# Moving the value products to the PSUM bank of the turned rows, and the residual behind the row sums, in a cross-attention and expert-layer kernel

## The reference

```python
q = layernorm(x) @ Wq + bq                     # 16 heads of 32
k, v = ctx @ Wk + bk, ctx @ Wv + bv            # 77 positions a batch
attn = softmax(clip(q k^T / sqrt(32), -1e4, 1e4))
x = x + (attn @ v) @ Wo + bo
weights = softmax over the top 2 of layernorm(x) @ expert_embeddings^T
each expert: its first 1024 rows with a weight, out = relu(rows @ W1^T) @ W2^T, times the weight
x = x + the experts' outputs, added into their rows
```

## Time and profile before

| | |
|---|---|
| time of the runs shown | median 1450.75 us (1443.56 to 1451.49, 3 runs) |
| profiled execution | 1449.84 us; span from the first to the last instruction 1448.1 us |
| busy over the span | PE 89%, DVE 67%, ACT 54%, POOL 49% |
| 120 to 657 us (beats 0 to 54) | of 537.00 us: PE 486.58, DVE 480.07, ACT 441.27, POOL 420.18 busy |
| 760 to 1448 us (the experts) | of 688.00 us: PE 670.48, DVE 328.46 busy |

### The profile page before, as it was taken

How to read it: one execution, slowest core, us unless ns; L and a number is a source line. 1 busy time by engine, 2 the same in 40 slices (tenths; PEclk the granted TensorE clock), 3 DMA queues, 4 the chain that set the end, 5 groups by cost and what they waited for, 6 DMA issues and landing times.

```text
span 1448.1 us, 33140 instructions
## 1 busy us (share of the span) xinstructions
PE 1293.5 (89%) x13650; PEld 741.0 (51%) x13650; DVE 973.5 (67%) x1909; ACT 778.2 (54%) x1272; POOL 716.6 (49%) x720
## 2 busy tenths in 40 slices
PE   6757898989999899987738999999999999999996
PEld 3535675656666666664417444444444444444442
DVE  8587898999989987897875545445554545455421
ACT  4467787867888788977345504234251514334210
POOL 3188788777777778876413333242513223241301
PEclk9878999999999999998858999999999999999998
DMA  7137898968798797898523665755747465654401
GB/s 224 45 84 159 215 243 204 250 174 200 194 224 203 150 206 175 191 209 196 147 54 138 177 166 155 154 169 126 185 110 184 137 155 175 148 145 121 107 15 44
DMA packets 320258, 230.12 MB, mean 159 GB/s; under 512 B 253465, under 2 KB 253849, under 8 KB 320106
## 3 DMA queue, kind: packets, MB, share of 16 engines
q1 hardware_dynamic: 304746, 177.33, 51.2%
q0 software_dynamic: 15360, 50.66, 11.9%
HBM read 120.04 MB, written 50.86 MB: 118 GB/s over the span
## 4 chain that ended last, share of the span: by engine, by line
PE 63%; DVE 14%; POOL 8%; ACT 5%; issue 5%; SPq 2%; DMA 1%; DVEq 0%; POOLq 0%; ACTq 0%
PE ps L1237 23%; PE ps L1223 23%; PE ps L1140 6%; PE ps L1070 4%; POOL sd L549 3%; PE ps L1121 2%; DVE ps L1462 1%; PE ps L1013 1%; POOL qT L531 1%; DVE sm L1491 1%; DVE x L1512 1%; DVE sd L1474 1%; POOL oT L537 1%; POOL ph L555 1%; ACT sd L756 1%
## 5 line engine op out<-in xcount | busy, mean ns | idle before, releaser
L1223 PE MATMUL ps<-xT,w1s 128*128 128x512 f16 (+1 forms) x1632 | 336.2, 368 | 1.9 <-DVE xT L1810 1.5
L1237 PE MATMUL ps<-w2s,hT 128*128 128x512 f16 x1536 | 332.8, 379 | 0.0
L852 ACT ACTIVATE hT<-ps 128x512 f16<-128x512 f32 (+1 forms) x136 | 77.8, 572 | 356.5 <-PE ps L1223 356.5
L1223 PEld LDWEIGHTS ps<-xT,w1s 128*128 128x128 f16 x1632 | 160.7, 99 | 175.3 <-issue 1.9
L1237 PEld LDWEIGHTS ps<-w2s,hT 128*128 128x128 f16 x1536 | 150.3, 98 | 181.3
L1070 PE MATMUL ps<-xnT,wqh 128*128 128x256 f16 x1536 | 197.0, 280 | 26.4 <-ACT partq L743 25.2
L600 POOL DMA_INDIRECT out_dram<-ys,idx x64 | 71.7, 1120 | 278.4 <-DVE ys L1850 273.9
L1140 PE MATMUL ps<-woh,oT 128*128 128x512 f16 x768 | 188.6, 392 | 16.5 <-POOL oT L537 14.0
L549 POOL TENSOR_TENSOR sd<-sd,rr 128x1232 f32<-128x1232 f32 x64 | 143.9, 2249 | 118.9 <-ACT rr L761 118.8
L1840 DVE SCALAR_TENSOR_TENSOR hT<-ps,hT 128x512 f16<-128x512 f32 (+1 forms) x136 | 88.7, 658 | 138.1 <-ACT hT L852 138.0
L1070 PEld LDWEIGHTS ps<-xnT,wqh 128*128 128x128 f16 x1536 | 148.6, 100 | 53.5 <-ACT partq L743 30.1
(11 more groups left out here) (226 smaller groups left out, 1894.7 us busy)
## 6 DMA issues: line engine op xcount, KB each, us to landing
xr<-x SPq DMA_DIRECT2D x64, 256.0 KB, 3.7
xrow_dram<-x SPq DMA_DIRECT2D x64, 256.0 KB, 3.8
out_dram<-x SPq DMA_DIRECT2D x64, 256.0 KB, 4.0
stage<-w1T SPq DMA_DIRECT2D x8, 2048.0 KB, 10.6
stage<-w2T SPq DMA_DIRECT2D x8, 2048.0 KB, 9.3
xt<-x SPq DMA_DIRECT2D x59, 256.0 KB, 3.6
xs<-x SPq DMA_DIRECT2D x56, 256.0 KB, 4.2
wqf<-wq SPq DMA_DIRECT2D x1, 1024.0 KB, 7.3
```

The costliest lines, as they stand in the source:

```text
L1223: ins = pe.matmul(hb[z][:, 0:wide], w1s[e % 2][:, a, k, ic * P:(ic + 1) * P], xT[:, 4 * b + k, cols], start=(k == 0 and i == 0), stop=(k = ...
L1237: ins = pe.matmul(yb[z][:, :], hT[:, a, k, s * P:(s + 1) * P], w2s[e % 2][:, b, k, :], start=(k == 0 and i == 0), stop=(k == 7 and i == 2))
```

## The change

Two things change. First, `pv_mm` writes to bank `bT` in every beat: it waits for the last reader of the turned rows (`tx_lo`, semaphore `xTl`), and the next `tx` waits for `o_hi` (semaphore `of`). `o_mm` is alone in `bA[0]` and waits for the residual before it (semaphore `x1`). Second, in beats before 55, DVE's `residual` and `oe_out` stand behind `s_recip` and `tx_lo`; and `add_slots` stands ahead of both sums.

```diff
@@ o_hi, on ACT
-                src = bA[1 if 2 * G + half >= TAIL + 2 else 0][:, :]
+                src = bT[:, :]
@@ pv_mm, on PE
-                if free[f"A{n}"]:
-                    pe.wait_ge(*free[f"A{n}"])
+                if free["T"]:
+                    pe.wait_ge(*free["T"])
...
-                        ins = pe.matmul(bA[n][strip, cols], vb[0:K, b, a, k, strip], pT[0:K, G % 2, d, c, :],
+                        ins = pe.matmul(bT[strip, cols], vb[0:K, b, a, k, strip], pT[0:K, G % 2, d, c, :],
...
-                free[f"A{n}"] = S["of"], 2 * G + half + 1
+                free["T"] = S["of"], 2 * G + half + 1
@@ the beats before the tail, on DVE
-                s_sum(h + 5, 0)
-                residual(h)
-                if h % 2:
-                    oe_out(h // 2)
                 if H:
                     add_slots(H)
+                s_sum(h + 5, 0)
                 s_sum(h + 5, 1)
...
                 s_recip(h + 5)
                 tx_lo(h + 11)
+                residual(h)
+                if h % 2:
+                    oe_out(h // 2)
                 ln2_stats(h)
```

More of the change, by code:

```diff
@@ L1096, in s_mm, with pv_mm @@
                 ins.then_inc(S["s"], 1)
-            def pv_mm(G, half, n=0):
+            def pv_mm(G, half):
                 if not 0 <= G < NG:
@@ L1288, in tensor @@
                 H = inverted_at(h)
-                pv_mm(G + 1, half, 1)
+                pv_mm(G + 1, half)
                 if half == 1:
```

## The result

The changed kernel takes 1461.64 us in the median of seven runs (1458.66 to 1468.45), the kernel before 1448.81 us in seven runs beside it (1443.56 to 1451.49). The ratio is 1.0098, with a 95% interval of 1.0076 to 1.0120: about 1% slower. The profiled execution of the changed kernel has a span of 1457.1 us against 1448.1 us, at the same mean clock of 0.959, so the profile shows 9.0 of the 12.8 us between the medians.

The account below looks back on a forecast made before the run. No engine stood out; the bound was a chain of waits through the even beats' value products. Terms 4.9 + 0 + 4.0 + 3.4 = 12.3 us on 1449.84 gave 1462.1, forecast 1463 us (own bounds 1457 to 1468, range 1450 to 1472).

Parts of the forecast that it names:

- the case given 0.55: Whole kernel: 12.3 us slower, a time of 1463 us with own bounds 1457 to 1468; chance 0.55.
- the rivals: Whole kernel: DVE's waits come back, 1441.8 (0.12); bank move hidden, 1454 (0.20); both beats pay, 1468 to 1475 (0.13).
- The residual's wait: On DVE: the prediction is wrong if this wait vanishes without another in its place.
- the hidden case: On PE: value products wait behind queries anyway, so only DVE's 3.4 us remain, 1454 us; chance 0.20.
- seven even beats with slots, without routing: Beats 26 to 30 and 40 to 46: value products begin 0.70 us later, 4.9 us in all.
- the odd beats beside them: Beside the seven: value products 0.28 us later but off the chain, taken as 0, other bound 2.0 us.
- eight even beats with slots and routing: Beats 32 to 38 and 48 to 54: value products also wait behind the routing steps, 4.9 us in all.
- give-back: Odd beats 39, 49, 51, 53: DVE's lost 0.83 us idling returns up to 2.6 us; net routing term 4.0.
- beats 1 to 25: Beats without slots: `tx_hi` waits and statistics directly behind the residual cost DVE 3.4 us, bounds 1.5 and 5.
- The new wait's latency: Every beat: from the end of `tx_lo` to the start of the value products pass 0.15 us.
- The chain: Beat 46: the last-ending waits run through the even beat's value products and enter the output products from POOL.
- `tx_hi`, the term that the forecast named itself: Odd routing beats: `tx_lo`, ahead of the residual, gets its input later, so part of the wait only changes name; unsized.

Follow-up runs that it names:

- experiment 1: The changed kernel with DVE's instructions back in the old order, so only the new banks remain: 1478.23 us, ratio 1.0182.
- experiment 4: The kernel before, same banks, with `residual`, `oe_out` and `add_slots` behind both sums but ahead of `value`, routing, reciprocals and `tx_lo`: 1440.92 us.
- experiment 11: The changed kernel's banks with DVE's order of experiment 4: 1458.88 us, ratio 1.0055 to the kernel before.
- both halves alone: Two runs against the kernel before: new banks with DVE's old order, 1478.23 us; DVE's new order with the old banks, 1491.94 us.
- experiment 5: Experiment 3 with `value` moved behind `tx_lo` and the residual: 1460.22 us, ratio 1.0068 to the kernel before.
- experiment 12: Experiment 3 with `value` as DVE's first instruction of the beat: 1467.66 us, ratio 1.0136 to the kernel before.
- experiment 3: The changed kernel with `add_slots` between the two sums instead of ahead of both: 1462.38 us, ratio 1.0088 to the kernel before.
- experiment 9: Experiment 3 with `value` as four `tensor_scalar` of 64 columns in place of one `tensor_tensor` of 256: 1473.16 us, ratio 1.0155.

## Why the prediction was right

The forecast was 1463 us and the measurement is 1461.64; the case given 0.55 came true, and the rivals fell. On the profiled executions, for which the sum was made, it gave 12.3 us and 9.0 were measured; the medians lie 12.8 us apart. The residual's wait did vanish, but nothing came back with it, since other waits of DVE, and in the odd routing beats held instructions, took its place. The bank move was not hidden: by itself it costs 28 us with the old order (experiment 1) and 18 with that of experiment 4 (experiment 11); nor did the change come near the 1454 us of that rival. The rule on rotating banks in the Trainium skill ("Perfetto Trace Analysis", section "Matmuls"), which the hidden case was weighed with, does not give this case's time: the new rotation is as long as the old one, but its reader is late in DVE's order.

Term by term, from lengths of beats in the two profiles:

| term | forecast | measured |
|---|---|---|
| seven even beats with slots, without routing | 4.9 | 1.7 |
| the odd beats beside them | 0 | -0.5 |
| eight even beats with slots and routing | 4.9 before give-back | 5.4 |
| the odd beats beside them (33 to 39, 49 to 53) | -0.9 | +1.6 |
| beats 1 to 25 | 3.4 | 1.8 |
| ahead of `score` of beat 0, and behind that of 54 | 0 | +0.7 and -1.7 |
| sum on the span | 12.3 | 9.0 |

These are lengths from one execution of each kernel, and PE's granted clock was low in different beats of the two (a mean of 0.86 in beats 2 and 10 after, in beat 4 before), so a few tenths of a us in a term may come from that alone.

- *The new wait's latency.* `tx_lo` ends at 586.20 + 0.63 = 586.83 and the value products begin at 586.97: 0.14 us, as from the earlier trace rows.
- *The chain.* That it enters the output products from POOL does not stand in the earlier trace rows; PE's timeline has it, where the second half of line 1140 in beat 46 waits 0.35 us for POOL's line 537.
- *Steady even beats with slots.* By the layout the value products of beat 46 come 0.70 us later; it was 2.97 - 2.36 = 0.61, and the pair lost 0.48. PE's idle time just ahead of them was forecast as some 0.7 us and was 0.34. Even without beat 28 the other six beats lost 0.4 us each, so 0.7 was too much. A second reason that the term came out small lies in the execution before. Beats 26 to 31, three of the seven pairs, are 0.7 us shorter in the changed kernel, as much as beat 28 alone, where PE's granted clock fell before and not after. Here is this beat by the windows view, before:

```profile
394.79:406.91 12.12, 10.01 (x161) 6.68 (x160) 8.21 (x17) 8.63 (x16) 9.07 (x7) 0.86 0.97 185
```

and after:

```profile
397.31:408.78 11.47, 9.04 (x165) 6.41 (x165) 8.22 (x17) 9.14 (x17) 9.87 (x7) 1.00 0.85 185
```

At a mean clock of 0.86 PE was busy for 10.01 us, at 1.00 for 9.04 with the same work. PE's 1 us more of busy time in the kernel before hides, by my estimate, about as much of the term. (The 12.50 us of beat 44 in experiment 4 have the same clock of 0.86.)
- *Routing beats.* The gross cost was near (5.4 for 4.9). What failed is the give-back. It was expected in beats 39, 49, 51 and 53, whose wait of 0.83 us ahead of the residual is gone, and these four are together 1.65 us longer. `tx_hi`, the term that the forecast named itself, is not the reason: DVE waits for it in none of the four. Instead one instruction of the routing is held in each. Line 1710 took 1.80 us instead of 0.18 (beat 39), line 1604 1.89 instead of 0.75 (49), line 1629 0.70 instead of 0.16 (51) and line 1670 1.50 instead of 0.18 (53). That is 4.6 us, against 3.3 us of waiting that went away: DVE, which no longer waits, comes to these instructions while POOL's line 555 still runs. Beat 39 before:

```profile
509.52 2.54 POOL L555 TENSOR_TENSOR ph<-sd,ph 128x1232 f16<-128x1232 f32 x1
512.26 0.18 DVE L1710 SCALAR_TENSOR_TENSOR colf<-ef,hcf 128x32 f32<-128x32 f32 x1
```

and after:

```profile
515.10 2.53 POOL L555 TENSOR_TENSOR ph<-sd,ph 128x1232 f16<-128x1232 f32 x1 [0.92 <-ACT ph L771]
515.89 1.80 DVE L1710 SCALAR_TENSOR_TENSOR colf<-ef,hcf 128x32 f32<-128x32 f32 x1
```

In beats 48 and 50 `score` waits 0.18 and 0.17 us for the scores, as forecast, and the value products wait 1.33 and 2.55 us, where over 2 us were forecast for beat 50.
- *Beats 1 to 25.* DVE waits for `tx_hi` 4.5 us in seven beats up to 265 us: 1.28 us in beat 3, 0.40 in beat 8. It is rarer and longer than the 0.2 us in ten beats that was forecast, and beats 1 to 25 lose 1.8 of the 3.4 us. The cover by other waits seems to have been larger than I took; no run shows this by itself.
- *What was not in the sum.* DVE's busy time in beats 1 to 54 rose by 11.9 us. More than half of it is longer instructions, most of them held: line 1721 took 9.3 us in all against 6.9, and the durations of routing and normalization add up to 73.9 against 69.2. No term of the forecast had this.

That the total came out right owes something to luck. The even beats with slots and the first beats were priced too high, the give-back of the odd beats did not come, and of the 12.8 us between the medians 3.8 are differences between executions. Shown are the direction and the place of the loss (the value products' wait behind `tx_lo`), by both halves alone, by experiment 11, and by experiments 5 and 12, which bring beats 44 to 47 back to within 0.2 us of the length of before, though not the whole kernel. That held instructions took the give-back is read from one trace of each kernel, and no run removes the holds alone. Open is how the 7 us of the beats with routing divide between the value products' wait and held instructions.

## What to carry to other kernels

When a group of products moves to another bank, find the instruction that reads the old contents out, and its place in the beat of its in-order engine: in this kernel this set when the group could start, though the number of banks was the same. If an instruction waits, move it only behind work that is ready earlier, and never behind a reader that others wait for; the residual behind both sums but ahead of `tx_lo` gained 9 us where the change lost 12.8. And before moving a short instruction whose operands lie in SBUF, look at what POOL does at the new place: in the changed kernel and in experiments 3, 5 and 12 what a move gained in one place was lost there again.

## What the runs showed of the hardware

An instruction of DVE can take many times its length with no wait shown. Line 1634 (16 columns) took 2.47 us beside POOL's line 555 (beat 19 before) and 0.25 us where line 555 was not running (beat 51 before). The 256 columns of line 1721 took 0.41 us alone, 0.87 to 1.56 us beside line 555 in experiment 3, of which 0.28 to 0.29 us came after POOL's end, 1.74 to 2.37 us beside line 549 in experiment 5, and 2.78 us in the worst place (beat 24 of experiment 12). The sums (line 1491) and the instructions that read PSUM (lines 1512 and 1457) kept their lengths within 0.1 us in beats 1 to 54 of every kernel here. `tensor_scalar` of 64 columns was held too: the first of a group of four took up to 1.33 us instead of 0.24 (experiment 9).
